# A decoder layer on one core: another order for h's transposes, exponentials and the attention's end, and a third buffer for the normalised rows

## The reference

```
def _layernorm(x): ...                      # over the 512 features, eps 1e-5
def _L0_attn_ref(x, w_qkv, w_swiglu, w_out):
    q, k, v = split(_rms(x) @ w_qkv.T)      # a running, normalised sum over the tokens
    w = exp(_rms(k))
    y = sigmoid(_rms(q)) * (cumsum(w * v) / (cumsum(w) + 1e-6))
    u, g = split(y @ w_swiglu.T)            # 2 x 2048
    return x + u * silu(g) @ w_out.T        # x here is the normalised x
def _L0_xattn_ref(Q, K, V, mask, w_q, w_k, w_v, w_o, b_o):
    # 32 query heads of 16, 8 groups of keys and values, causal, padding mask
    attn = softmax(masked(q @ k.T / 4))
    return (attn @ v) @ w_o.T + b_o         # keys and values come from ctx
def _L0_ffn_ref(x, gate_w, w1, w2, w3, ws1, ws2, ws3):
    scores = softmax(xf @ gate_w.T)         # 8 experts
    weights, idx = top_k(scores, 2)
    y = sum over the two picks of weights * ((silu(xf @ w1.T) * (xf @ w3.T)) @ w2.T)
    z = (silu(xf @ ws1.T) * (xf @ ws3.T)) @ ws2.T      # the shared expert
    return y + z
x = x + _L0_attn_ref(_layernorm(x), ...)
x = x + _L0_xattn_ref(_layernorm(x), ctx, ctx, ...)
x = x + _L0_ffn_ref(_layernorm(x), ...)
```

## Time and profile before

| | |
|---|---|
| three runs | 1401.96, 1407.77, 1408.48 us; median 1407.77 |
| the profiled execution | 1406.43 us, of which the span (first to last instruction) is 1404.7 us |
| granted TensorE clock, mean | 0.987 |
| busy | PE 96%, weight loads 76%, DVE 58%, ACT 43%, POOL 37% of the span |

### The profile page before, as it was taken

One profiled execution on the slowest core, in us unless ns is written; L12 is line 12 of the kernel. 1 busy time (PEld: TensorE's weight loads), 2 busy tenths in 40 slices (PEclk: granted clock), 3 DMA queues, 4 the chain that ended last, 5 costly groups with the idle time before them and its releaser, 6 DMA issues.

```text
span 1404.7 us, 23677 instructions
## 1 busy us (share of the span) xinstructions
PE 1346.8 (96%) x8180; PEld 1072.4 (76%) x8180; DVE 819.7 (58%) x2085; ACT 607.9 (43%) x1135; POOL 515.2 (37%) x485
## 2 busy tenths in 40 slices
PE   8999999999999999999999999999988999999994
PEld 6788888888888888888877777777766887777662
DVE  5888765333333333333457787787776476666662
ACT  4444441111111111111127677777776223777772
POOL 4555442202020202020427654446453112565643
PEclk9999999999999999999999999999999899999997
DMA  6000012010010101010100000000011824465653
GB/s 255 1 0 0 0 42 94 0 45 26 21 45 1 45 0 45 0 46 0 49 27 2 20 21 20 21 20 3 5 47 59 351 86 157 85 110 93 106 97 45
DMA packets 20533, 73.41 MB, mean 52 GB/s; under 512 B 2320, under 2 KB 3344, under 8 KB 18000
## 3 DMA queue, kind: packets, MB, share of 16 engines
q0 software_dynamic: 10176, 25.17, 9.2%
q1 hardware_dynamic: 10256, 46.93, 9.0%
HBM read 52.95 MB, written 19.14 MB: 51 GB/s over the span
## 4 chain that ended last, share of the span: by engine, by line
PE 85%; DVE 6%; issue 3%; ACT 2%; DMA 2%; POOL 2%; DVEq 0%; POOLq 0%; ACTq 0%
PE ps L781 21%; PE ps L783 21%; PE ps L782 21%; PE ps L1029 6%; PE ps L1214 5%; PE ps L1021 2%; DVE den L1640 2%; PE ps L1053 2%; PE ps L1121 1%; PE ps L1018 1%; DMA h_rows<-hd 1%; PE ps L1047 1%; PE ps L1184 1%; POOL cols L673 1%; ACT cols L1434 1%
## 5 line engine op out<-in xcount | busy, mean ns | idle before, releaser
L781 PE MATMUL ps<-feat,wsplit 128*128 128x512 f32 (+1 forms) x672 | 247.2, 368 | 3.2 <-PE ps L783 2.2
L783 PE MATMUL ps<-feat,wsplit 128*128 128x512 f32 (+1 forms) x672 | 244.7, 364 | 0.0
L782 PE MATMUL ps<-feat,wsplit 128*128 128x512 f32 (+1 forms) x672 | 244.6, 364 | 0.0
L1291 ACT ACTIVATE sg<-ps 128x512 f32<-128x512 f32 x64 | 38.3, 598 | 368.8 <-PE ps L783 368.8
L1560 DVE TENSOR_TENSOR m_f<-ps,sg 128x512 f32<-128x512 f32 x64 | 44.2, 691 | 245.3 <-ACT sg L1291 245.3
L541 POOL CAST wsplit<-wraw 128x3072 fp32r<-128x3072 f32 x9 | 24.8, 2754 | 399.3 <-PEq L969 386.6
L1828 DVE CUSTOM_DVE_ANT_0 cols<-ps,msk 128x256 f32<-128x256 f32 (+1 forms) x512 | 146.1, 352 | 28.8 <-PE ps L1021 16.6
L781 PEld LDWEIGHTS ps<-feat,wsplit 128*128 128x128 f32 x672 | 126.7, 189 | 26.3 <-issue 6.6
L783 PEld LDWEIGHTS ps<-feat,wsplit 128*128 128x128 f32 x672 | 126.8, 189 | 20.1
L782 PEld LDWEIGHTS ps<-feat,wsplit 128*128 128x128 f32 x672 | 126.8, 189 | 19.6
L1422 ACT COPY cols<-ps 128x512 f32<-128x512 f32 x192 | 110.9, 578 | 61.2 <-PE ps L1029 61.2
(11 more groups left out here) (281 smaller groups left out, 3023.9 us busy)
## 6 DMA issues: line engine op xcount, KB each, us to landing
wraw<-weights SPq DMA_DIRECT2D x11, 1536.0 KB, 6.5
rawx<-weights SPq DMA_DIRECT2D x8, 1536.0 KB, 12.8
ctx_raw<-ctx_t SPq DMA_DIRECT2D x8, 512.0 KB, 4.6
h_rows<-hd POOLq DMA_DIRECT2D x16, 256.0 KB, 2.7
out<-acc SPq DMA_DIRECT2D x4, 1024.0 KB, 4.3
qkv_raw<-weights SPq DMA_DIRECT2D x6, 512.0 KB, 6.9
acc<-x SPq DMA_DIRECT2D x1, 3072.0 KB, 17.0
acc<-x SPq DMA_DIRECT2D x2, 512.0 KB, 6.8
```

Source lines behind the costliest of these rows:

```text
L781: nc.tensor.matmul(out_, w_hi, m_hi, start=first, stop=False)
L782: nc.tensor.matmul(out_, w_lo, m_hi, start=False, stop=False)
L783: return nc.tensor.matmul(out_, w_hi, m_lo, start=False, stop=last)
```

## The change

Four things change. `TURNED` puts the transposes of h to units 3 and 6 (from 1 and 2), with kT and v, and so shifts the banks of the pieces. ACT makes the exponentials of unit u - 2 in unit u (before: u - 1). At the attention's end the `attend` of set 4 stands between p0 and p1, and hT1's skipped turn goes. `hd` has three buffers, with their semaphores; `h_d(2)` and `h_d(3)` stand ahead of the first two lo parts on DVE. Small tables of the router that lay behind `hd` now lie within its place.

```
+HDS = 3
-TURNED = {1: "hT0", 2: "hT1"}
+TURNED = {3: "hT0", 6: "hT1"}
...
-        hd = at("hd", [P, 2, D], F32)
+        hd = at("hd", [P, HDS, D], F32)
...
+        tri8 = at("tri8", [P, EXPERTS, EXPERTS], F32)
+        steps16 = at("steps16", [P, TILES], F32)
+        picked = at("picked", [P, TOP * TILES, EXPERTS], F32)
+        ends = at("ends", [P, COLS, EXPERTS], F32)
         assert place[0] <= d_end, (place[0], d_end)
-        tri8 = at("tri8", [P, EXPERTS, EXPERTS], F32, off=d_end)
...
-        h_stored = [sem(f"d_h_stored{k}") for k in range(2)]
+        h_stored = [sem(f"d_h_stored{k}") for k in range(HDS)]
...
-                pool.dma_start(h_rows[t * P:(t + 1) * P, :], hd[:, t % 2, :]).then_inc(h_stored[t % 2], 16)
+                pool.dma_start(h_rows[t * P:(t + 1) * P, :], hd[:, t % HDS, :]).then_inc(h_stored[t % HDS], 16)
...
             turned_piece("p0", BATCH)
-            turned_piece("hT0", BATCH)
+            attend(BATCH - 1, 4)
             turned_piece("p1", BATCH)
-            attend(BATCH - 1, 4)
             head_t(0)
             head_t(1)
-            turned_piece("hT1", BATCH)
             turned_piece("p2", BATCH)
+            turned_piece("hT0", BATCH)
             turned_piece("p3", BATCH)
...
                 for u in range(UNITS):
-                    if u >= 1:
-                        exps(b, u - 1)
+                    if u >= 2:
+                        exps(b, u - 2)
                     elif b > 0:
-                        exps(b - 1, UNITS - 1)
+                        exps(b - 1, UNITS - 2 + u)
...
+            exps(BATCH - 1, UNITS - 2)
+            turned_read("p0", BATCH)
             exps(BATCH - 1, UNITS - 1)
-            turned_read("p0", BATCH)
             turned_read("p1", BATCH)
...
             def h_d(t):
                 dve.wait_ge(d["rstd"], t // TPG + 1)
-                after(dve, d["hT_ps"], t - 1)
-                after(dve, h_stored[t % 2], 16 * (t // 2))
+                after(dve, d["hT_ps"], t - HDS + 1)
+                after(dve, h_stored[t % HDS], 16 * (t // HDS))
...
+            h_d(2)
+            h_d(3)
             hT_lo_d(0)
             hT_lo_d(1)
-            h_d(2)
-            h_d(3)
```

More of the change, by code:

```diff
@@ L301, in decoder_layer @@
         lane_tile = at("lane_tile", [P, 2, TOP * TILES], F32)
+        tri8 = at("tri8", [P, EXPERTS, EXPERTS], F32)
+        steps16 = at("steps16", [P, TILES], F32)
+        picked = at("picked", [P, TOP * TILES, EXPERTS], F32)
+        ends = at("ends", [P, COLS, EXPERTS], F32)
         assert place[0] <= d_end, (place[0], d_end)
-        tri8 = at("tri8", [P, EXPERTS, EXPERTS], F32, off=d_end)
-        steps16 = at("steps16", [P, TILES], F32, off=d_end + 256)
-        picked = at("picked", [P, TOP * TILES, EXPERTS], F32, off=d_end + 320)
-        ends = at("ends", [P, COLS, EXPERTS], F32, off=d_end + 320 + 1024)
         lanes = at("lanes", [P, TOP * TILES, P], F32R, off=acc_at)
@@ L759, in _ @@
             pool.wait_ge(d["zero"], 32)
-            for k in range(2):
-                pool.wait_ge(h_stored[k], 16 * (TILES // 2))
+            for k in range(HDS):
+                pool.wait_ge(h_stored[k], 16 * ((TILES + HDS - 1 - k) // HDS))
             pool.wait_ge(x_stored[2], 16)
@@ L1111, in head_t @@
                     pe.wait_ge(d["h"], g + 1)
-                    source = hd[:, g % 2, :]
+                    source = hd[:, g % HDS, :]
                 else:
@@ L1871, in h_d @@
                 dve.wait_ge(d["rstd"], t // TPG + 1)
-                after(dve, d["hT_ps"], t - 1)
-                after(dve, h_stored[t % 2], 16 * (t // 2))
-                nc.vector.tensor_scalar(hd[:, t % 2, :], acc[:, t, :], mv_d[:, t, 0:1], ln_d[:, t, 1:2], ALU.subtract, ALU.mult).then_inc(d["h"], 1)
+                after(dve, d["hT_ps"], t - HDS + 1)
+                after(dve, h_stored[t % HDS], 16 * (t // HDS))
+                nc.vector.tensor_scalar(hd[:, t % HDS, :], acc[:, t, :], mv_d[:, t, 0:1], ln_d[:, t, 1:2], ALU.subtract, ALU.mult).then_inc(d["h"], 1)
             def hT_lo_d(g):
@@ L1938, in slot_bases @@
             def slot_bases():
-                for k in range(2):
-                    dve.wait_ge(h_stored[k], 16 * (TILES // 2))
+                for k in range(HDS):
+                    dve.wait_ge(h_stored[k], 16 * ((TILES + HDS - 1 - k) // HDS))
                 dve.wait_ge(d["hT_ps"], TILES)
```

## The result

The changed kernel takes 1391.41 us, the median of four runs (1390.23 to 1394.46), beside 1408.12 for the kernel before on the same chip: a ratio of 0.9894, 95% interval 0.9862 to 0.9927. The profiled execution took 1392.23 us, 14.2 less than that of before, with a span of 1390.5 us and a mean granted clock of 0.992. The forecast of 1392.4 us holds, but its terms do not all hold: two came out larger and one, the attention's end, was lost. Most lines after line 73 stand one further down than before, those of ACT in a pass where they stood (`probs_t` 1030, `turn_h` 903, `attend` 1048 and 1054, `scores` 1019 and 1022, `head_t` 1122, the logits 1143, `h_d` 1875, `hT_lo_d` 1880).

What follows compares the result with a forecast made beforehand. PE, busy 96% of the span, bounds the kernel, so only its waits and half-clock time can go: 3.3 + 1.6 + 0.6 + 1.65 + 1.8 + 5.1 = 14.05 us off 1406.43 gives 1392.4 us; range 1387 to 1400.5.

Steps and rivals of the forecast that it cites:

- the attention's end: Behind the last pass: `attend` fills PE's wait, tile 3's row comes just in time; 1.65 us less, bounds 0 and 3.4.
- Logits' wait and half-speed stretch: Experts' stage: three buffers end PE's 1.8 us wait on the logits; without that pause full clock saves 5.1 us.
- The rule against it: Stores share 16 DMA engines, so a third slows them: at 10.8 us each, PE waits 0.4 us instead of 1.8.
- rival (a): Logits: clock falls again or store is late, 1397.5 to 1399.3 us; gain 9 against runs without the stretch; chance 0.17.
- Six changes of batch: PE's waits before p1 and hT1, 1.04 us each time, become 0.4 to 0.5 before hT0; 3.3 us less for six.
- First batch: From hT0 to p6: a 2.35 us wait for DVE's maxima replaces one of 3.25; 1.6 us less taken.
- upper case: First batch, clock staying up after the pause: 2.5 us less, against 0.8 if it falls.
- Last pass: One bank clash goes, one comes; copies no longer stand behind exponentials lacking maxima; 0.6 us less, bounds 0 and 4.4.
- (b): The attention gains nothing, since ACT is the late engine at each change of batch: 1399.5 us, chance 0.12.
- (c): Slower: PE's transposes wait for the later exponentials, 20 us over eight passes: 1412.8 us, chance 0.05.
- (d): Whole kernel: nothing changes, the waits just move; 1406 us, chance 0.04.
- The sign of being wrong that `scores` waits for maxima: Attention, trace after: the prediction is wrong if `scores` waits for maxima in each set; no size given.

## Why the prediction was right, and where it was not

**Logits' wait and half-speed stretch, 1.8 + 5.1: right.** 6.9 predicted, 6.86 measured, and the buffer alone gives it. The mechanism holds as told, a store's wait with `router_max` queued behind it: moving the copy ahead of the wait gives the same with two buffers. The rule against it, in the Trainium skill (DMA: Bandwidth & Descriptors, "Issuing engines are not separate DMA queues"), had its price worked out from stores half as long again, 10.8 us. They landed after 7.4 us in the median in the same stretch, before 7.2, so that no run here bears out that price. What was not foreseen is how loosely the clock's fall hangs on the wait: a wait of 1.78 us left the clock at 1.00 in the kernel with two buffers, one of 1.54 in that with the exponentials alone. The size of 5.1 us is that of executions in which it falls, as in the profiled one of before. Before's runs seem to show both: those on the third chip lie at 1402.2 to 1404.9 (mean clock 0.990 to 0.991) and at 1407.4 to 1411.6 us (0.985 to 0.987); no profile of the lower group shows where its clock stayed up. Beside the 1393.2 of the changed kernel there, the middle of the lower group (1403.6) gives a gain of 10, where rival (a) had named 9 for such runs, that of the upper (1409.8) one of 17. That is what rival (a) held possible by the Trainium skill (TensorE: Matmul & The Clock Gate, "What's actually happening"), and the two profiles of the changed kernel agree with the rule: one with half clock in the first batch, one without, behind the same wait of 2.10 us.

**Six changes of batch, 3.3: right in mechanism, too small; 5.07 measured.** hT0 starts 3.07 us after p0 (855.18 to 858.25); by the prediction's own times it was 3.0 to 3.1 (860.35 to 863.35 and 0.1). What was mis-sized is the loss that it takes the place of. The old waits of 0.67 and 0.37 are counted from modelled ends; by the starts and the 0.55 us of a group, which the new times were worked out with, the old one before p1 is 0.78 (860.86 + 0.55 = 861.41 to 862.19). The new wait is 0.39 in that measure (857.31 + 0.55 = 857.86 to 858.25), 0.29 in the row's. 0.78 + 0.37 - 0.39 = 0.76 a pass, where 0.55 was taken. Most of the rest of the 0.85 is hT1's group: it held PE for 0.54 us ahead of p2 (864.19 to 864.73) and holds it for 0.41 ahead of the value products (863.82 to 864.23). Here the prediction says of the exponentials only that they cost PE nothing; its times hold only with them two behind, for one behind the wait before hT0 is 1.06 us.

**First batch, 1.6: right by its upper case.** The wait for the maxima is 2.10 us where 2.35 was expected, and the gain is 2.35 where 2.5 was named for a clock that stays up. The 1.6 lay between that and 0.8 with a fall, and in the second profile, with one, 12.07 - 10.93 = 1.14 are left. So about half of the 2.35 is luck of the clock.

**Last pass, 0.6: right,** 0.53. It comes from the exponentials, as told: they alone bring the pass from 36.65 us to 35.87, and the other edits with them one behind bring it to 37.25. DVE's maxima hold back part of what the banks give; without the skipped turns it takes 35.57, 0.55 less than in the changed kernel.

**The attention's end, 1.65: this step failed.** It gave 0.12, and then 1.05 were lost behind it at half clock. The wait of p3 is as predicted (1.04 us for 1.0). The failing part is the sentence that tile 3's row "needs tile 0's store and holds the low part of tile 0 behind it on DVE to about 1072.2, just in time", 5.67 us after p0. The prediction shows no row for that store. With a store that is issued 1.7 us after p0, as in both traces, and lands in 2.4 us, as the first of the pair does in before, the part would be ready some 5.3 us after p0 (1.7 + 2.4 + 0.5 + 0.7, an estimate with the durations of the row and the part); this store took 4.0. The lo parts of tiles 0 and 1 started at 1063.75 and the first ended near 1064.4, 7.0 us after p0, and `head_t(2)` waited 1.20 us for it. With two buffers, where no row of tile 3 stands ahead of the lo parts, nearly the same order of PE's pieces took 7.00 us in the kernel with the places alone and 7.52 in the changed kernel with two buffers, where before takes 8.62. It is the same fault as the one that the third buffer mends in the logits: a wait for a store with a step of the critical path queued behind it. Moving the row behind the lo parts gave the gain back (8.50 to 6.73 us, 7.44 with a store of 4.4 us), and the clock stayed up in all five profiles that have the move. The 1.05 us at half clock behind the stretch were not foreseen; before lost none there, though its order of the end does so in other profiles (see the last section). The other part of the step, that `attend` fills the wait for p1, was right in its times (it starts 1.28 us after p0, 1.27 predicted) but not in its worth: p1 has its other bank free by then too, and behind p1 `attend` does as well.

**The sum** of 14.05 came out as 14.2 partly by luck: the passes and the first batch gave 2.5 us more than their terms, the end 2.6 us less (0.12 - 1.05 against 1.65). **The rivals:** (b), that the attention gains nothing, is refuted by 0.85 us a pass; (c), that exponentials become what PE waits for, by waits of 3.6 us for ACT before transposes of probabilities where 10.9 stood; (d) by the result. (c)'s sum of 1406.4 + 20 - 14 is 1412.4, not 1412.8, which changes nothing. The sign of being wrong that `scores` waits for maxima showed only in the first batch and the last pass, not in each set.

## What to carry to other kernels

A wait for a slow transfer costs what is queued behind it on its engine: look for what the critical path needs there and put it ahead, before adding a buffer, and look again at every place where an added buffer lets such a wait move forward. Where two queues share banks in turn, cost an edit of the order together with what the emptying engine does between its copies; here the places alone gave 0.09 us a pass, the exponentials alone 0.47 and both 0.85. Price old and new waits in the same measure, from start to start, and where a stretch at half clock follows a wait, cost it for executions with and without it.

## What was not expected of the hardware

- **A store of 256 KB takes 2.4 to 5.0 us to land where only one or two of its kind run beside it.** The first store at the attention's end landed in 2.4 us in the kernels of before, of the buffer alone, of the exponentials alone and of the moved copy, in 3.1 and 3.9 us in the two others that issue two there, and in 3.0 to 4.4 us in the eight that issue three. In before the second of the pair took 5.0 us; in the changed kernel all three took 3.8 to 4.0. So a third store isn't needed for the longer time, and its cause is open.
- **The clock's fall is not bound to a wait's length.** Behind the same waits it came in some executions and not in others: 1.78 us before the logits without a fall and 1.80 with 10.2 us at half clock; 2.10 us in the first batch without and with 3.41 us. Seven profiles run the first batch as the changed kernel does, with that wait of 2.10 us; three have the fall. At the attention's end it came in both profiles of the changed kernel, behind waits of 1.04 and about 1.2 us, and in none of the five with tile 3's row later (1.00 in each). But it didn't come with the exponentials one behind, where nearly the same waits stand:

```profile
1071.66 1.23 PE L1122 MATMUL ps<-ident,hd 128*128 128x128 f32 x8 [1.14 <-DVE hT_first L1879]
```

There the clock is 1.00 from p0 to the wait for `oT`. And with the end in its old order it came behind the wait of 1.93 us in two profiles (the exponentials alone, the moved copy) and not in the two others (before, the buffer alone). So the fall is not the changed kernel's own, and that moving the row prevents it is likely by five profiles, not proven.
